# Cross attention: the values of two key tiles in one visit to 32-column matmuls

## The reference

```python
def _mha_cross(q_in, kv_in, in_w, in_b, out_w, out_b):
    ...
    scores = jnp.einsum('bhqd,bhkd->bhqk', q, k) / jnp.sqrt(jnp.float32(Dh))
    p = jax.nn.softmax(scores, axis=-1)
    out = jnp.einsum('bhqk,bhkd->bhqd', p, v).transpose(0, 2, 1, 3).reshape(B, S, D)
    return out @ out_w.T + out_b
```

## Time and profile before

| | us |
|---|---|
| median of the runs | 3099.2 |
| lowest, highest | 3093.8, 3110.6 |
| profiled execution | 3103.9 |
| its span | 3102.2 |
| TensorE busy | 2968.8 (96%) |
| VectorE busy | 1734.2 (56%) |
| GpSimd busy | 1856.8 (60%) |
| ScalarE busy | 1257.9 (41%) |

### The profile page before, as it was taken

The page is one execution under the profiler, slowest core; times in us unless marked ns, Lnnn a source line. Parts: engine busy times, 40 slices in busy tenths (PEclk is TensorE's granted clock), DMA queues, the critical chain, the costliest instruction groups (busy, mean ns, idle before and its releaser), DMA issues.

```text
span 3102.2 us, 39671 instructions
## 1 busy us (share of the span) xinstructions
PE 2968.8 (96%) x15346; PEld 1962.3 (63%) x15346; DVE 1734.2 (56%) x2849; ACT 1257.9 (41%) x2359; POOL 1856.8 (60%) x968
## 2 busy tenths in 40 slices
PE   9999999999999988999999999999989999999998
PEld 7888886444444446764444444444458888888887
DVE  5455656777777755767777777777632222212220
ACT  3122222555555534446666666666632111111111
POOL 5223333788888837548888888888947334333422
PEclk9899999999999989999999999999999999999999
DMA  8455764555455337742342432422140101001000
GB/s 274 153 157 182 237 210 130 111 110 110 110 111 110 96 105 227 226 137 56 73 92 55 89 77 59 102 59 66 49 146 14 41 28 41 25 30 41 28 14 14
DMA packets 199794, 310.18 MB, mean 100 GB/s; under 512 B 15267, under 2 KB 93619, under 8 KB 199603
## 3 DMA queue, kind: packets, MB, share of 16 engines
q1 hardware_dynamic: 199606, 307.64, 36.3%
HBM read 189.04 MB, written 117.44 MB: 99 GB/s over the span
## 4 chain that ended last, share of the span: by engine, by line
PE 82%; DVE 9%; POOL 3%; issue 3%; DMA 2%; ACT 1%; SPq 0%; DVEq 0%; POOLq 0%; ACTq 0%
PE p_ring L89 14%; PE m_ring L89 14%; PE m_o_ps L89 11%; PE e_st L1325 8%; PE e_pv L1337 7%; PE e_nat L1308 7%; PE b_pv L1337 4%; PE b_st L1325 4%; PE c_ring L89 4%; PE b_nat L1308 3%; DVE b_nat L1215 3%; PE e_st L1352 3%; DVE e_neg_max L1218 2%; PE b_st L1352 2%; POOL e_probs L1162 1%
## 5 line engine op out<-in xcount | busy, mean ns | idle before, releaser
L1162 POOL TENSOR_TENSOR e_probs<-e_probs 128x2048 f32<-128x2048 f32 x155 | 709.8, 4587 | 123.8 <-ACT e_probs L1137 119.4
L1218 DVE TENSOR_REDUCE e_neg_max<-e_nat 128x1 f32<-128x1024 f32 x512 | 602.9, 1216 | 173.7 <-PE e_nat L1308 168.7
L1137 ACT ACTIVATE e_probs<-e_st 128x512 f32<-128x512 f32 x1024 | 557.9, 598 | 345.1 <-PE e_st L1325 327.4
L1137 ACT ACTIVATE b_probs<-b_st 128x512 f32<-128x512 f32 (+3 forms) x768 | 341.3, 491 | 292.9 <-PE b_st L1325 282.4
L1215 DVE CUSTOM_DVE_ANT_0 b_nat<-b_nat,mask_qk 128x128 f32<-128x128 f32 (+7 forms) x512 | 374.1, 783 | 80.8 <-PE b_nat L1308 79.5
L1325 PE MATMUL e_st<-e_qs,e_ks 98*128 98x512 f32 x1024 | 394.1, 428 | 11.4 <-DMA e_qs<-e_max_lo 7.8
L1662 POOL TENSOR_TENSOR m_hid_lo<-m_hid,m_hid_hi 128x512 fp32r<-128x512 f32 x128 | 168.3, 1315 | 368.1 <-DVE m_hid_hi L1702 368.1
L1702 DVE CAST m_hid_hi<-m_hid 128x512 fp32r<-128x512 f32 x128 | 56.5, 441 | 579.7 <-ACT m_hid L1578 579.7
L1162 POOL TENSOR_TENSOR b_probs<-b_probs 128x1536 f32<-128x1536 f32 (+3 forms) x120 | 351.2, 2927 | 36.1 <-PE b_pv L1337 33.6
L1308 PE MATMUL e_nat<-e_ks,e_qs 96*128 96x512 f32 x1024 | 327.0, 400 | 22.1 <-DVE e_neg_max L1218 13.5
L1325 PEld LDWEIGHTS e_st<-e_qs,e_ks 98*128 98x128 f32 x1024 | 175.0, 188 | 262.5 <-ACT e_probs L1137 192.8
(11 more groups left out here) (198 smaller groups left out, 5292.0 us busy)
## 6 DMA issues: line engine op xcount, KB each, us to landing
b_qs<-sq_hi SPq DMA_DIRECT2D x32, 512.0 KB, 6.2
b_ks<-sk_hi SPq DMA_DIRECT2D x32, 512.0 KB, 11.6
e_qs<-cq_hi SPq DMA_DIRECT2D x32, 512.0 KB, 6.8
e_ks<-ck_hi SPq DMA_DIRECT2D x32, 512.0 KB, 12.3
ck_hi<-p_part_hi SPq DMA_DIRECT2D x32, 256.0 KB, 3.6
ck_lo<-p_part_lo SPq DMA_DIRECT2D x32, 256.0 KB, 3.6
cv<-p_tok_out SPq DMA_DIRECT2D x32, 256.0 KB, 3.2
p_x<-in_x SPq DMA_DIRECT2D x8, 1024.0 KB, 7.4
```

The lines of the kernel that those rows point to most:

```text
L1137: act.activation(probs[:, home(n, k), j, first:TOK], st_ps[:, bank_at("scores", blk), first:TOK], ACT.Exp).then_inc(exped, 1)
L1162: pool.tensor_tensor(into, into, probs[:, home(n, k), :, first:TOK], ALU.add).then_inc(added, 1)
L1218: dve.tensor_reduce(neg_max[:, u:u + 1], found, AX.XY, ALU.max, negate=True).then_inc(maxed, 1)
```

## The change

In cross attention, `weigh` is no longer called in each step: `due` gives nothing in even steps and both tiles, k - 1 and k, in odd ones, and the visit stands at head 3 instead of 2. The sums move one step back, to steps 11 and 3, so that they stay in a visit; `invert` and `normalise`, which count from `sum_at`, move with them. Units of maxima stand at heads 0 and 2 of each step; 0, 2 and 3 in a step with sums; 2 alone in the step behind it. TURN_HEAD becomes 0 and PE_TURN_HEAD 2, so the transpose stands one head earlier, and six units instead of four of a set belong to the set before the last. Self attention keeps its order.

```diff
-    TURN, TURN_HEAD, PE_TURN_HEAD, TURN_BANK = NS - 3, 2, 2 if causal else 3, 2
+    TURN, TURN_HEAD, PE_TURN_HEAD, TURN_BANK = NS - 3, 2 if causal else 0, 2, 2
...
-    sum_at = {h: last_step[h] + LATE + 3 for h in range(HALVES)}
-    VISIT_HEAD = 2
+    PAIRED = not causal
+    VISIT_HEAD = 3 if PAIRED else 2
+    sum_at = {h: last_step[h] + LATE + (3 if not PAIRED else 2 if causal else 4) for h in range(HALVES)}
+
+    def due(at):
+        last = at - LATE
+        if PAIRED:
+            return (last - 1, last) if last >= 1 and last % 2 == 1 else ()
+        return (last,) if last >= 0 else ()
...
-            beside = [j for h in range(HALVES) for j in ((0, 1, 2) if sum_at[h] % NS == k else
-                                                         (0,) if (sum_at[h] + 1) % NS == k else ())]
-            slots += [k * HG + j for j in beside or (0, 1)]
+            beside = [j for h in range(HALVES) for j in ((0, 2, 3) if sum_at[h] % NS == k else
+                                                         (2,) if (sum_at[h] + 1) % NS == k else ())]
+            slots += [k * HG + j for j in beside or (0, 2)]
...
-                            if n * NS + k >= LATE:
-                                weigh(*divmod(n * NS + k - LATE, NS))
+                            for at in due(n * NS + k):
+                                weigh(*divmod(at, NS))
...
-            for k in range(NS - LATE, NS):
+            for k in range(NS - LATE * (2 if PAIRED else 1), NS):
```

## The result

The changed kernel takes 3108.4 us (median of 20 runs, 3103.4 to 3113.1), the kernel before 3101.7 (20 runs, 3093.8 to 3110.6). The ratio is 1.0023, with a 95% interval of 1.0016 to 1.0029: slower by 7 us, a quarter of one per cent, and within the half per cent that counted as no change. The forecast had been 3104, which is +5.1 on the median of 3099.2 that I had at hand; on the 3101.7 measured here the same sum gives 3106.8. The profiled execution has a span of 3110.5 us.

The account below looks back on a forecast made before the run. TensorE was taken to bound the kernel (82% of the chain), with VectorE's maxima able to hold it. Sets +4.3, late sets -1.5 and early row +2.3 gave +5.1 on 3099.2: 3104 us, own range 3092 to 3115, overall 3078 to 3122.

Parts of the forecast that it names:

- The bound and the prices: Cross attention: TensorE busy 55.35 of 56.54 us a set; hand-layout prices include 1.85 for a visit of 16 matmuls.
- the plain double step: Two cross-attention steps sharing one visit of 16 matmuls, four a set: 6.17 us laid out, against 6.13 before.
- behind the sums: Steps 4 and 5, after a visit with row sums: three pairs, third e_st waits for the bank; 5.93 us.
- merging is worth 0.33 a visit, and VectorE's buffers eat it: Cross attention: each visit saved gives 0.33 us, 2.7 a set, but pairs waiting for VectorE's maxima use it up.
- The first rival: In cross attention, waits for maxima stay at 10.6 us in 14 sets: about 3059 us, chance 0.17.
- the slower one: In cross attention, the second of two maxima starts 1.28 behind the first, not 1.14: 15 us, 3119, chance 0.13.
- The sum per set: Cross-attention set laid out at 56.85 us against 56.54: 0.31 more in each of 14 sets, +4.3.
- The two late sets: Two cross-attention sets where e_st waited for the DMA of the split maxima lose 0.76 us each: -1.5.
- The early row: Before cross attention, six maxima of the second set instead of four run in one row at VectorE's 1.13: +2.3 us.
- The sign for TensorE's idle time: Idle time before e_nat from VectorE rises from 10.6 us in 14 sets to 30 or more in over 100 places.
- ScalarE's cover: In the plain double step, the fourth exponential frees the seventh e_st's bank at 2.86, before its place at 3.09: 0.2.
- The rule weighed: Inside each merged visit, a same-row weight load that cannot overlap costs about 0.11 us: +12, 3116, chance 0.02.

Follow-up runs that it names:

- head 3: Changed kernel with the second pair of maxima of each odd step without sums moved one head later, behind that step's last scores: 3105.3 us, ratio 1.0009.
- the even spread: Changed kernel with row sums first in their visit and maxima at heads 0 and 2 of even, 1 and 3 of odd steps: 3080.4 us, 0.9936.
- the fastest version: Changed kernel, maxima at heads 0 and 2 of even, 0 and 3 of odd steps, row sums first, early units two by two: 3073.0 us, 0.9911.

## Why the prediction was right

Point by point, by its own steps.

**The bound and the prices** held. A merged visit is 1748.85 to 1750.70, 1.85, as costed; the long one 1762.07 to 1766.50, 4.43 against 4.44; third and fourth pairs of the plain double step at 2.28 and 3.41 against 2.28 and 3.42; the double step 6.16 against 6.17 and 5.96 against 5.93 behind the sums (1738.58 to 1744.54). The set was laid out at 56.85 and takes 56.80. This is the mechanism that the prediction named, and not only its number.

**That merging is worth 0.33 a visit, and VectorE's buffers eat it**, is shown from both sides: with halved maxima a plain double step falls from 2 x 3.07 = 6.14 to 5.87, 0.27 of the 0.33, and the whole merge gains 14.1 us; at the old places it loses 31 us. The first rival (visits count, holds don't, 3059) fell with the plain double step, and the slower one (3119) with the 1.13 between third and fourth pair.

**The sum per set**, +0.31, is +0.26 in the two rows shown. The two late sets are gone, as costed. Over 14 sets that was +4.3 - 1.5 = +2.8, and the traces have +2.4.

**The early row** was mis-sized: +2.3 was costed, and the stretch from the transpose to the first e_st grew by 3.9 (13.46 to 17.37). The two more units follow at VectorE's 1.13, as costed; what the sum left out is the clock behind them, 0.43 instead of 0.23 for eight matmuls, 1.6 us. In the profiled pair the span grew by 8.3: 1.9 ahead of the transpose, where no instruction differs and the clock was lower, 3.9 here, 2.4 in the sets, and 0.1 in all from the first e_st on outside them. Without the first of these that is 6.4 against the 5.1 summed, and the medians differ by 6.8.

**The sign for TensorE's idle time** was wrong. The prediction wanted 30 us or more before e_nat in over 100 places; PE's row has 4.5 in 27. The mechanism is there, in the row of PEld (65.0 in 196). A stand shorter than the modelled tail of a matmul doesn't show as idle time of PE.

**ScalarE's cover** of 0.2 was counted as enough. For this change it was, since the double step came out as laid out, with VectorE's holds in front of the critical e_st. But the bank is wanted by the weight load, which in these traces starts 0.23 ahead of its matmul, so a cover of 0.2 against the matmul's place is none. When the experiments moved the pairs, my layouts missed plain double steps by 0.14 (head 3) and 0.19 (heads 1 and 3). That the 0.14 are ScalarE's is shown by the halved exponentials; for the 0.19 that run was not made.

**The rule weighed.** Weight loads in a visit of 16, in the changed kernel:

```profile
1742.68 0.16 PEld L1348 LDWEIGHTS e_pv<-e_probs,e_vs 128*32 128x32 f32 x8 [0.37 <-ACT e_probs L1148]
1743.14 0.13 PEld L1348 LDWEIGHTS e_pv<-e_probs,e_vs 128*32 128x32 f32 x4 [0.30 <-ACT e_probs L1148]
1743.57 0.13 PEld L1348 LDWEIGHTS e_pv<-e_probs,e_vs 128*32 128x32 f32 x4 [0.30 <-issue]
```

The loads of the third and fourth rounds of four stand at 1743.14 and 1743.57, 0.43 apart, right behind the starts of the rounds before, and the visit takes the 1.85 costed without any exposed load. The Trainium skill (TensorE: Matmul & The Clock Gate, Part 3) lets loads overlap only where the row group differs. These share it, and the trace does not agree. But the same part also lets a load run ahead when it goes to the array's background weight buffer. No run here shows where a load goes; by that clause the trace would be as expected, and the rule weighed was only half of what the part says.

## What to carry to other kernels

Fewer switches between two kinds of work mean longer stretches of each, and an engine with two buffers that rests through one kind must catch up in the other: lay the new order out against each buffer, instruction by instruction, before counting the switches saved. Count a release from the weight load, not from the matmul: here 0.03 us of lateness cost 0.14. And look at the order inside a stretch first: in the merged kernel the row sums ahead of the weighting brought 8 us and the even spread 20 more, and the two together brought 18 us to the kernel before (3100.2 on that chip), where merging is worth some 5.

## What was not expected of the hardware

- Four stands of 0.85, 0.40, 0.40 and 0.40 us in 5 us, with pairs between, were followed by 3 us at a granted clock of 0.50, in each of the four versions that have this row; with the stands broken up the clock stayed at 1.00 over 27 us. Each version is one profiled execution. What brings the 0.72 at 1357 to 1363 stays open; seven of fourteen traces show such a fall there, with and without the row.
- A release of a score bank that comes late by little costs 0.14 of TensorE's time and leaves next to nothing in PE's own waits (2.2 us in 7 waits, against 57.4 in 212 for the loads, in the fastest version).
